# A five-layer graph network on one Trainium2 core: the adjacency matrix loaded in quads of four tiles instead of pairs

## What is computed

```
# layer 0: a row's last 100 neighbours, the latest with weight 1, halved at each step back
rank = cumsum(adj != 0, axis=1); deg = rank[:, -1:]; k = min(deg, 100)
pos  = rank - (deg - k)
w    = mask * where(pos > 0, 0.5 ** (k - pos), 0)
x = norm(x + w @ (x @ W0) + b0)
# layer 1: two gated steps, each:  m = adj @ (x @ W), then a GRU cell of (m, x); relu
x = norm(x + ggc(ggc(x)))
# layer 2: deg = rowsum(adj + I);  x = norm(x + (D^-1/2 (adj + I) D^-1/2 x) @ W2)
# layer 3: x = norm(x + concat(x, adj @ x / (deg + 1)) @ W3.T)
```

## Time and profile before

| | us |
|---|---|
| median of 3 runs | 430.13 (429.86 to 430.8) |
| the profiled execution | 430.51 |
| its span, first to last instruction | 428.7 |
| PE busy | 404.7 |
| DVE busy | 295.4 |
| ACT busy | 215.1 |
| POOL busy | 116.8 |

### The profile page before, as it was taken

How to read it: one execution, slowest core, us unless ns; L and a number is a source line. 1 busy time by engine, 2 the same in 40 slices (tenths; PEclk the granted TensorE clock), 3 DMA queues, 4 the chain that set the end, 5 groups by cost and what they waited for, 6 DMA issues and landing times.

```text
span 428.7 us, 6431 instructions
## 1 busy us (share of the span) xinstructions
PE 404.7 (94%) x2243; PEld 191.2 (45%) x2258; DVE 295.4 (69%) x862; ACT 215.1 (50%) x345; POOL 116.8 (27%) x154
## 2 busy tenths in 40 slices
PE   5878989999999999998999999999999999999991
PEld 2332433434344444444555555555554444445480
DVE  3377968867976787473964566776949566477773
ACT  2566788688868877506864554635222121212100
POOL 8213223231420100015231304234325434311111
PEclk9998999999999999999999999999999999999997
DMA  8999999999999994173011110000000101100000
GB/s 144 108 115 106 107 107 108 107 108 107 109 107 107 107 108 44 44 95 67 20 42 33 38 32 6 8 7 2 0 2 13 27 12 26 26 14 26 25 26 13
DMA packets 26241, 24.68 MB, mean 58 GB/s; under 512 B 14776, under 2 KB 17624, under 8 KB 26208
## 3 DMA queue, kind: packets, MB, share of 16 engines
q0 software_dynamic: 9360, 16.78, 39.1%
q1 hardware_dynamic: 16704, 7.41, 8.0%
q10 hardware_dynamic: 144, 0.07, 0.1%
HBM read 69.32 MB, written 1.06 MB: 164 GB/s over the span
## 4 chain that ended last, share of the span: by engine, by line
PE 80%; DMA 7%; DVE 4%; POOL 2%; issue 2%; ACT 1%; SPq 1%; POOLq 0%; DVEq 0%; ACTq 0%
PE Y L1099 45%; PE both L1008 15%; DMA adjT<-in_adjT 6%; PE both L987 3%; PE Y L987 3%; PE both L1015 3%; PE both L999 2%; PE Y L999 2%; PE both L959 2%; SPq L281 1%; PE both L955 1%; PE both L957 1%; POOL rstd L305 1%; POOL adjT L333 1%; DMA work<-x 1%
## 5 line engine op out<-in xcount | busy, mean ns | idle before, releaser
L1099 PE MATMUL Y<-adjT,S 128*128 128x512 fp8e4 (+1 forms) x1056 | 231.0, 373 | 0.8 <-DVE S L587 0.8
L1099 PEld LDWEIGHTS Y<-adjT,S 128*128 128x128 f16 x1056 | 101.8, 98 | 109.0 <-DVE S L587 0.9
L417 ACT ACTIVATE wgt<-both,consts 128x512 int16<-128x512 f32 x160 | 106.9, 687 | 33.6 <-PE both L1008 29.9
L305 POOL TENSOR_TENSOR rstd<-stat,mhalf 128x4 f32<-128x4 f32 (+2 forms) x29 | 35.1, 1212 | 149.1 <-DVE stat L527 149.1
L1008 PE MATMUL both<-adjT,tri 128*128 128x512 fp8e4 x160 | 61.3, 384 | 2.9 <-DMA adjT<-in_adjT 2.7
L1008 PE MATMUL both<-adjT,fix 128*128 128x512 fp8e4 x152 | 58.4, 384 | 2.3 <-ACT wgt L417 1.1
L333 POOL DMA_DIRECT2D adjT<-in_adjT x63 | 36.9, 593 | 78.8 <-DMA adjT<-in_adjT 78.8
L547 DVE SCALAR_TENSOR_TENSOR work<-Y,yT 64x512 f32<-64x512 f32 x30 | 20.8, 695 | 47.6 <-ACT yT L376 47.4
L376 ACT ACTIVATE yT<-Y 64x512 f32<-64x512 f32 x30 | 17.6, 587 | 65.2 <-PE Y L1099 41.6
L320 POOL TENSOR_TENSOR S<-work,S 128x256 f16<-128x256 f32 x24 | 18.8, 785 | 48.0 <-ACT S L401 27.4
L387 ACT ACTIVATE work<-work 64x512 f16<-64x512 f32 x30 | 18.8, 627 | 26.1 <-DVE work L547 24.6
(11 more groups left out here) (129 smaller groups left out, 477.6 us busy)
## 6 DMA issues: line engine op xcount, KB each, us to landing
adjT<-in_adjT POOLq DMA_DIRECT2D x63, 256.0 KB, 39.0
work<-x SPq DMA_DIRECT2D x16, 64.0 KB, 2.0
out_rows<-xrow SPq DMA_DIRECT2D x7, 128.0 KB, 1.9
xrow<-in_xrow SPq DMA_DIRECT2D x1, 640.0 KB, 7.2
x<-in_w_gates SPq DMA_DIRECT2D x1, 512.0 KB, 5.8
biases<-in_biases SPq DMA_DIRECT2D x1, 384.0 KB, 4.2
x<-S SPq DMA_TRANSPOSE x24, 2.4
xrow<-in_xrow SPq DMA_DIRECT2D x1, 256.0 KB, 3.6
```

The source lines that it names most:

```text
L305: nc.gpsimd.tensor_tensor(rstd[:, 0:blocks], stat[:, 2, 0:blocks], mhalf[:, 0:blocks], ALU.pow)\
L417: nc.scalar.activation(wgt[:, c, tiles % 2, :], V[c][:, :], ACT.Relu, bias=tile_bias[sums]).then_inc(w_ready[c], 1)
L1099: mm = nc.tensor.matmul(bank(layer, g)[:, 0:nb * P], S[layer % 2][:, jb, :], cols[:, jb, :], start=(jb == 0), stop=(jb == JB - 1), skip_gr ...
```

## The change

The matrix is loaded in quads: 32 transfers of 512 KB, the first cut into the first tile and the other three. `NLOAD` is 8, which keeps the same number of bytes in flight. The order is by whole quads: 7, 6, 5, ... 0 in stage 0, and 6, 7, 5, ... 0 in the others. In DRAM the array is laid out so that a partition's row of a quad is contiguous (`in_adjT` has quads where it had pairs). PE waits for a landing at the first tile of a quad alone (31, 23, 15, 7, 3) and, at the very first quad, at tile 30. SP's two waits and POOL's `root` are put at the places that answer to the old ones. `BETWEEN` is a new table.

```diff
--- before.py
+++ after.py
@@ -27,7 +27,7 @@
 B = GC // P
 Q = G // 2
 JP = JB // 2
-NLOAD = 16
+NLOAD = 8
 MAX_NEIGH = 100
 STEP = 128
 KEEP = 127 * STEP
@@ -216,15 +216,15 @@
         UNITS[-1][-1:] = [(JB - B, B // 2), (JB - B // 2, B // 2)]
 
         ORDER = [
-            [15, 14, 13, 12, 11, 10, 9, 8, 5, 7, 6, 4, 3, 2, 1, 0],
-            [13, 12, 15, 14, 11, 10, 9, 8, 7, 6, 5, 4, 3, 2, 1, 0],
-            [13, 12, 15, 14, 11, 10, 9, 8, 7, 6, 5, 4, 3, 2, 1, 0],
-            [13, 12, 15, 14, 11, 10, 9, 8, 7, 6, 5, 4, 3, 2, 1, 0],
+            [7, 6, 5, 4, 3, 2, 1, 0],
+            [6, 7, 5, 4, 3, 2, 1, 0],
+            [6, 7, 5, 4, 3, 2, 1, 0],
+            [6, 7, 5, 4, 3, 2, 1, 0],
         ]
 
         def landing(q, pair):
 
-            return q * JP + ORDER[q].index(pair)
+            return q * G + ORDER[q].index(pair // 2)
 
         def in_halves(layer, g):
 
@@ -249,14 +249,14 @@
             for i, (lo, hi) in enumerate(X_PARTS):
                 sp.dma_start(xrow[:, lo * B:hi * B, :], a["xrow"][:, lo * B:hi * B, :]).then_inc(x_in[i], 16)
             sp.dma_start(bias0, a["biases"][:, 0:D].to_broadcast([P, D])).then_inc(bias0_in, 16)
-            sp.wait_ge(load[3], 16)
+            sp.wait_ge(load[1], 16)
             sp.dma_start(w_y[:, :], a["w_y"]).then_inc(w_y_in, 16)
             for q in range(Q):
                 for c in range(2):
                     sp.wait_ge(deg_picked[c], q + 1)
                     c0 = (2 * q + c) * GC
                     sp.dma_start(deg_rows[:, c0:c0 + GC], deg_row[c][0:1, :]).then_inc(row_out[c], 16)
-            sp.wait_ge(load[14], 64)
+            sp.wait_ge(load[6], 64)
             sp.wait_ge(dsum_used, Q * NM)
             sp.dma_start(biases[:, D:13 * D], a["biases"][:, D:13 * D].to_broadcast([P, 12 * D])).then_inc(biases_in, 16)
             sp.dma_start(gate_pack, a["w_gates"]).then_inc(gate_in, 16)
@@ -320,18 +320,18 @@
                 nc.gpsimd.tensor_tensor(s[:, :, D:2 * D], ts[:, :, :], s[:, :, 0:D], ALU.subtract).then_inc(s_ready, 1)
 
             for q in range(Q):
-                for n in range(JP):
-                    i = q * JP + n
+                for n in range(G):
+                    i = q * G + n
                     if i >= NLOAD:
                         pool.wait_ge(load[i % NLOAD], 16 * (i // NLOAD))
-                    jp = ORDER[q][n]
+                    quad = ORDER[q][n]
                     if i == 0:
-                        for half, landed in ((1, first_tile), (0, load[0])):
-                            pool.dma_start(adjT[:, q, 2 * jp + half, :], a["adjT"][q, jp][:, 2 * GC * half:2 * GC * (half + 1)])\
+                        for lo, hi, landed in ((B - 1, B, first_tile), (0, B - 1, load[0])):
+                            pool.dma_start(adjT[:, q, B * quad + lo:B * quad + hi, :], a["adjT"][q, quad][:, 2 * GC * lo:2 * GC * hi])\
                                 .then_inc(landed, 16)
                     else:
-                        pool.dma_start(adjT[:, q, 2 * jp:2 * jp + 2, :], a["adjT"][q, jp]).then_inc(load[i % NLOAD], 16)
-                    if q >= 2 and n == 5:
+                        pool.dma_start(adjT[:, q, B * quad:B * (quad + 1), :], a["adjT"][q, quad]).then_inc(load[i % NLOAD], 16)
+                    if q >= 2 and n == 2:
                         root(q - 2, 2 * B)
             root(Q - 2, 2 * B)
             root(Q - 1, 2 * B)
@@ -1024,11 +1024,11 @@
                 nc.tensor.matmul(V[0][:, :], cutw[:, :], ones[:, :], start=True, stop=True)
             pe.wait_ge(const_ready, 3)
             BETWEEN = (
-                {(1, 0): ((8,),), (4, 0): ((13,),), (7, 0): ((6, 3, 0), (6, 3, 1)), (8, 0): ((6, 2, 0), (6, 2, 1)), (8, 1): ((6, 1, 0), (6, 1, 1)), (9, 0): ((6, 0, 0), (6, 0, 1)), (10, 0): ((3,),), (15, 1): ((4, 3, 0), (4, 3, 1)), (16, 1): ((4, 2, 0), (4, 2, 1)), (17, 0): ((4, 1, 0), (4, 1, 1)), (17, 1): ((4, 0, 0), (4, 0, 1)), (20, 0): ((2, 3, 0), (2, 3, 1)), (20, 1): ((2, 2, 0), (2, 2, 1)), (21, 0): ((2, 1, 0), (2, 1, 1)), (21, 1): ((2, 0, 0), (2, 0, 1))},
...
+                {(1, 0): ((20,),), (4, 0): ((7,),), (6, 0): ((6, 3, 0), (6, 3, 1)), (6, 1): ((6, 2, 0), (6, 2, 1)), (7, 1): ((6, 1, 0), (6, 1, 1)), (8, 0): ((6, 0, 0), (6, 0, 1)), (10, 0): ((3,),), (15, 0): ((4, 3, 0), (4, 3, 1), (4, 2, 0), (4, 2, 1)), (16, 0): ((4, 1, 0), (4, 1, 1)), (17, 0): ((4, 0, 0), (4, 0, 1)), (19, 0): ((2, 3, 0), (2, 3, 1)), (19, 1): ((2, 2, 0), (2, 2, 1)), (20, 0): ((2, 1, 0), (2, 1, 1)), (20, 1): ((2, 0, 0), (2, 0, 1))},
...
             )
 
             def slot(q, s, c):
@@ -1055,9 +1055,9 @@
                         slot(q, s, 0)
                         if kind == "tile":
                             i = landing(q, at // 2)
-                            if i == 0 and at % 2 == 1:
+                            if i == 0 and at % B == B - 1:
                                 pe.wait_ge(first_tile, 16)
-                            elif i == 0 or at % 2 == 1:
+                            elif at % B == B - 1 or i == 0 and at % B == B - 2:
                                 pe.wait_ge(load[i % NLOAD], 16 * (i // NLOAD + 1))
                         for c in range(2):
                             if c == 1:
@@ -1313,7 +1313,7 @@
         lifts[:, NM + 1 + i] = (i + 1) * QUAD_TOTAL - CUT
     arrays = {
 
-        "adjT": flat(adj.reshape(Q, 2 * GC, JP, 2, P).transpose(0, 2, 4, 3, 1)).reshape(Q, JP, P, 4 * GC),
+        "adjT": flat(adj.reshape(Q, 2 * GC, G, B, P).transpose(0, 2, 4, 3, 1)).reshape(Q, G, P, 2 * B * GC),
         "xrow": flat(x.reshape(JB, P, D).transpose(1, 0, 2)),
         "consts": flat(np.concatenate([tri, lifts], axis=1)),
         "w_y": flat(np.concatenate([w_y, w_y], axis=0)), "w_gates": w_gates, "biases": biases,
```

## The result

| us | before | after |
|---|---|---|
| median | 430.0 (429.52 to 430.8, 4 runs) | 427.62 (427.3 to 427.74, 4 runs) |
| the profiled execution | 430.51 | 427.54 |
| its span | 428.7 | 425.7 |
| POOL's last operation ends | 423.08 | 422.72 |
| POOL's last DRAIN ends | 428.48 | 425.50 |

The ratio is 0.9938, with a 95% interval of 0.9925 to 0.9951. The kernel before has one run more here than in the table ahead of the prediction, hence 430.0 and not 430.13.

What follows compares the result with a forecast made beforehand. PE and its chain with ACT were taken to bound layer 0 after quad 3 of stage 0, the load slightly ahead. Terms 1.45 + 0.1 - 1.5 - 0.1 = -0.05 gave a median of 430.1 us, range 429.2 to 431.6.

Steps and rivals of the forecast that it cites:

- Covered: Work hidden elsewhere, counted as nothing: POOL's 32 fewer issues of 0.53 us, `root`'s delay, SP's waits, one next-layer product.
- Stage 0 up to quad 2: Start of layer 0: no change, since quad 3 is awaited until 33.6 in both kernels and empty matmuls fall inside waits.
- Quad 1 of stage 0: Its first count comes 1.65 us late, less 0.86 of masked products done meanwhile: +0.8 at the end of stage 0.
- First tile of stage 1: Tile 31 waits for whole quad 7 until 58.2; step 1 begins at 59.4, not 57.94: +1.45 us, including stage 0's 0.8.
- Quad 3 of stage 1: PE comes to it near 73.0 and it lands at 73.1: +0.1 us.
- Fewer waits in lockstep: Stages 1 to 3: 0.5 us from waits dropped at steps 2 and 7, 1.0 from masked products at 10 and 15: -1.5.
- Larger transfers: The load's pace with transfers twice as large: -0.1 us, staying by the mean of 2.46 us between pair landings.
- One product inside layer 0, at no cost: One product of the next layer moves from behind layer 0 to inside it, costing 0.216 us in either place.
- three signs of being wrong: Whole-quad landings over 0.5 us off, stages not shrinking by 0.5 each, or the clock falling elsewhere than near 34.
- A: Rival, slower: late first tile stands and waits give nothing back, 431.7; or a clock fall, 431.3; chance together 0.25.
- B: Rival, faster: larger rows shorten the load by the full 2%, stage 1 starts at most 0.85 earlier, 429.3; chance 0.15.
- C: Rival: larger transfers are slower or come in lumps, +1.1 us at the start of stage 1, 431.2; chance 0.08.

Runs made afterwards that it cites:

- e3: The kernel after with one more drain on POOL, behind the last `root` of layer 0; 427.06 us, ratio 0.9925 to the kernel before.
- e4: The kernel before with one more drain on POOL, behind the last `root` of layer 0; 426.91 us, ratio 0.9922 to the kernel before.
- e6: The kernel after with the products ahead of the first count of steps 10 and 15 in stages 1 to 3 put behind it; 428.97 us, ratio 0.9964.
- e9: The kernel after with PE's waits at every odd tile restored and the products at steps 10 and 15 put behind the first count; 429.14 us, ratio 0.9972.
- e1: The kernel after with each quad as two transfers on one semaphore, 65 issues; 430.91 us, ratio 1.0017 to the kernel before.
- e2: The kernel after, one transfer per quad but each partition's row cut into two of 2048 elements, 34 transfers; 428.13 us, ratio 0.9947.

## Why the prediction was wrong, step by step

**The step that failed is in *Covered*:** "POOL makes 32 issues of 0.53 us fewer, but it is never late". True of its issues; but each issue leaves something behind that POOL's closing DRAIN has to settle, 0.083 us apiece, and that drain stood alone at the end of the program: 32 x 0.083 = 2.66 us where the sum has zero; the traces have 5.40 against 2.78, 2.62. The rows were there in the trace of before: a DRAIN of 6127 ns on POOL from 422.3, and every engine's closing event at 428.6 with SP through at 425.3, 3.3 us of idle end. The sum asked of each microsecond inside the layers what hides it, and never asked what ends the program. With -2.66 in it the forecast is 427.4, and the median came out at 427.62.

**What was right, and what came out by luck.** Up to the last operation -0.05 was forecast; the trace has -0.36, the profiled execution of before standing 0.5 above its median, and e3 against e4, the same comparison with the drain out of the way, has +0.15 in the medians and 0 in the traces. The amount is about right, but its terms are not all; the errors cancel in part:

- *Stage 0 up to quad 2*: as said. Quad 3 is awaited until 33.51 (1.26 us of idle time), the empty matmuls lie inside waits.
- *Quad 1 of stage 0, +0.8*: the quad is counted at 43.08 and not 43.5, and the stage is 0.4 to 0.6 longer. The second masked pair waited 0.60 for DVE, as was allowed for.
- *First tile of stage 1, +1.45 in all*: the count ran at 57.68 and not 58.2, with 0.59 of idle PE before it, step 1 at 58.84 where it was 57.94: +0.90, of which 0.41 had come up by stage 0's last product (56.28 to 56.69, forecast 0.8) and 0.49 behind it. The chain behind the count, count to count, took 1.16 as worked out. What was mis-sized is the landing: 58.2 was forecast, and it came at 57.63.
- *Quad 3 of stage 1, +0.1*: nothing is awaited, thanks to the masked products in the hole. Quad 1 of stage 1 has no term, though it would be awaited without them (0.56 in e6).
- *Fewer waits in lockstep, -1.5*: the waits gave 0.45 over three stages (forecast 0.5). The masked products gave 0.14 and 0.17 in stages 2 and 3, half of the forecast 0.34 each, and in stage 1 their gain is one with the two hidden landings. Both together are worth 0.87 + 0.30 + 0.31 = 1.48 by e9. That this meets the forecast's 1.5 is luck: if stage 1 had no late landing and gained as the other two do, it would be 0.9 (an estimate from the 0.30 and 0.31), and the rest is work done while a landing is due, which the term did not mean.
- *Larger transfers, -0.1*: POOL's issue at tile 31 of stage 1 is 0.56 earlier than in the trace of before (0.3 from the middle of one group of runs to that of the other) and 1.15 earlier fourteen quads on, by a pace of 4.89 and not 4.93; the -0.1 had no row behind it. The Trainium skill, "DMA: Bandwidth & Descriptors", section "Anatomy of one DMA — SWDGE (gpsimd) path", gives each transfer a fixed cost of about 2.0 us. It is not to be seen in this pace: with rows of one length it is 4.94 with 65 transfers and 4.93 with 34 (e1 and e2), and the 1% came with the longer rows.
- *One product inside layer 0, at no cost*: true in sum, and it explains a stage. The table has one product fewer in stage 1, two more in stage 2 and one fewer behind layer 0: -0.22, +0.43, -0.22 at 0.216 each. Stage 2 gained 0.30 by the waits and masks and paid 0.43 for the two products, which would be +0.13; it came out at +0.04, and stage 3 gained 0.40 where these two give 0.31. So 0.09 in each stage is not accounted for; other entries of the table moved as well, and no run tries them. The 0.23 behind stage 3 is the third product.

**The signs.** Stage 3's end (178.32 for 178.45), the wait until 33.5 and 0.216 ahead of the masked products came as said. So did all three signs of being wrong: tile 31 landed 0.57 early, the three stages shrank by 0.19, -0.04 and 0.40 and not by 0.5 each, and the clock did not fall near 34. They tell that the terms inside layer 0 were off; none of them looks at the end of the program.

**The rivals.** A did not come: the waits did give back, and the granted clock is 1.00 from 56 to 97. B named the faster side for another reason, a load that is 2% quicker; it is 1%, and e2, which lacks it, is 0.5 slower than the kernel after, with intervals that overlap. C did not come either: the larger transfers land earlier. That the time would come out faster for something that isn't in layer 0 was no rival at all, and a range built from cases inside layer 0 could not hold it.

**What stays open:** whether the change without its drain loses 0.1 or gains 0.1; e3 against e4 can't tell it. This near zero also holds some 0.7 us that the kernel before loses to the clock in stage 0 and the kernel after does not (last section). What the drain does in its 0.083 us for each transfer isn't shown either, only that packets don't count.

## What to carry to other kernels

Read the end of the program before summing up its middle: the closing instructions of each engine, and which of them the others wait for. This kernel, whose transfers are issued by POOL, paid for each at its last drain; one drain of its own, behind the last landing and in a gap of POOL, takes that off the end (3.3 us in the kernel before and 0.6 in the kernel after, for one line), but the same line among transfers in flight stops the load. When a time changes, ask for the last operation's time first: if it stood still, the cause lies behind the work.

## What the hardware showed that was not expected

- POOL's DRAIN costs 0.083 to 0.087 us for each transfer that POOL has issued since its last DRAIN (16, 33, 34 and 65 of them), whether they landed long ago or not, and independent of packets; those in flight it waits for. The Trainium skill, "VectorE: DVE Perf Modes", section "The DRAIN you can't avoid", has the closing DRAINs of all five engines at a constant of about 12 ns. SP's are like that (7 and 13 ns); POOL's of 6127 ns is not. ACT's, DVE's and PE's (414, 328 and 700 ns in the kernel before) are longer than 12 ns too, but they are over by 423.5.
- The stretch of half clock, 1.2 GHz among 2.4, moves about, and it has a price in one place. In the profile of after it lies in the empty matmuls that follow the first tile, from 9.84 to 13.25:

```profile
9.84:13.25 3.41, 3.41 (x10) 1.21 (x9) 0.00 (x0) 0.72 (x2) 0.09 (x1) 0.50 0.97 96
```

There it costs nothing that shows: e3 has none before 56 and ends stage 0 at 57.48, after at 57.38, since until quad 3 of stage 0 PE waits for the load anyway. Behind 33.5 it is otherwise. Both traces of the program of before have it there, after 2.15 us of idle time and 2.01 in e4; no trace of the kernel after or its variants does, where PE had been idle for 1.66 at most. The window of the earlier trace rows in e4, then in e3:

```profile
33.50:40.00 6.50, 6.28 (x21) 1.97 (x22) 3.66 (x8) 4.67 (x7) 3.14 (x3) 0.74 1.07 107
```

```profile
33.50:40.00 6.50, 5.44 (x24) 1.83 (x25) 4.48 (x12) 4.92 (x8) 1.06 (x2) 1.00 1.04 109
```

From quad 3's first count to the last product of step 14, the same matmuls in all of them, it takes 7.76 us in the kernel before (33.66 to 41.42), 7.85 in e4, 7.19 in the kernel after (0.38 of it a wait for DVE) and 6.64 in e3. The pair that the next count of the kernel before needs landed at 41.05 (POOL's issue at 41.33, less 0.28), and the count ran at 41.81; in e4 it landed at 40.84 and was counted at 41.59. So some 0.7 us are lost to the clock there, an estimate. The prediction measured its +0.8 for quad 1 from that late count, and named the clock only as something that the change could bring. What stage 0 of the kernel before would be without the fall has not been tried.
